# Layer norms' rows moved from VectorE to ScalarE, the second experts' gate made one SiLU, and new priorities for the order of the work

## What is computed

```python
h = _layernorm(x, axis=-1) * (1 + ca) + sa
x = x + ga * _L0_attn_ref(h, ...)      # 8 heads, top 20% of the scores emphasised
h = _layernorm(x, axis=-1) * (1 + cb) + sb
x = x + gb * _L0_ffn_ref(h, ...)       # two more layer norms inside, 8 experts, SiLU
...
h = _layernorm(x, axis=-1) * (1 + ca) + sa
x = x + ga * _L1_attn_ref(h, ...)      # state-space scan, 16 states
h = _layernorm(x, axis=-1) * (1 + cb) + sb
x = x + gb * _L1_ffn_ref(h, ...)       # 8 experts of limited capacity
```

```python
h = jnp.einsum('eti,eih->eth', einp2, w_c_fc) + b_c_fc
g = jnp.einsum('eti,eih->eth', einp2, w_gate) + b_gate
o = jnp.einsum('eth,eho->eto', jax.nn.silu(h * g), w_c_proj) + b_c_proj
```

## Time and profile before

| | us |
|---|---|
| median of 3 runs (lowest, highest) | 2912.05 (2910.93, 2914.12) |
| the profiled execution, whole | 2906.13 |
| its span in the trace | 2904.7 |
| DVE busy | 2341.4 (81%) |
| PE busy | 2152.1 (74%) |
| ACT busy | 1467.0 (51%) |
| POOL busy | 1193.4 (41%) |

### The profile page before, as it was taken

One profiled execution on the slowest core, in us unless ns is written; L12 is line 12 of the kernel. 1 busy time (PEld: TensorE's weight loads), 2 busy tenths in 40 slices (PEclk: granted clock), 3 DMA queues, 4 the chain that ended last, 5 costly groups with the idle time before them and its releaser, 6 DMA issues.

```text
span 2904.7 us, 33586 instructions
## 1 busy us (share of the span) xinstructions
PE 2152.1 (74%) x8658; PEld 1109.6 (38%) x8767; DVE 2341.4 (81%) x6145; ACT 1467.0 (51%) x3124; POOL 1193.4 (41%) x1118
## 2 busy tenths in 40 slices
PE   4168776978788876877778876878778787778644
PEld 2016322643244522553245522554235532454214
DVE  5974898988898898988898888988988887953472
ACT  3306814775276714765166723766156741744323
POOL 2020354515363353615454153814445163724461
PEclk8579898998989999998989899998979899889757
DMA  4011013232132313242142312233033321313223
GB/s 107 1 24 38 26 31 105 78 100 68 40 124 57 114 42 93 70 107 78 31 126 67 100 49 79 91 86 96 24 111 77 97 61 46 116 44 107 81 74 97
DMA packets 137459, 215.11 MB, mean 74 GB/s; under 512 B 17872, under 2 KB 57440, under 8 KB 134112
## 3 DMA queue, kind: packets, MB, share of 16 engines
q1 hardware_dynamic: 133088, 203.88, 24.8%
q0 software_dynamic: 4096, 8.40, 1.0%
HBM read 190.06 MB, written 22.15 MB: 73 GB/s over the span
## 4 chain that ended last, share of the span: by engine, by line
DVE 37%; issue 19%; PE 17%; POOL 11%; ACT 9%; DVEq 4%; another core or an unknown queue 2%; DMA 1%; SPq 0%; POOLq 0%; ACTq 0%
DVE wmask L819 9%; DVE best L961 6%; POOL gat L1670 4%; ACT wmask L801 4%; DVEq L963 4%; PE ps_att L1079 3%; POOL slots L1786 2%; POOL rest_c L1683 2%; DVE pick L968 1%; DVE xr L1914 1%; PE ps_rest L1457 1%; PE ps_att L1090 1%; PE ps_rest L1371 1%; PE ps_rest L1831 1%
## 5 line engine op out<-in xcount | busy, mean ns | idle before, releaser
L1431 POOL TENSOR_TENSOR gat<-sil,cbs 128x512 f32<-128x512 f32 x256 | 325.2, 1276 | 432.9 <-ACT sil L1396 371.2
L1396 ACT ACTIVATE sil<-ps_rest,w_b1T 128x512 f32<-128x512 f32 x256 | 175.4, 686 | 471.5 <-PE ps_rest L1371 438.1
L819 DVE TENSOR_SCALAR_CACHE_REDUCE wmask<-z,tc 128x512 bf16<-128x512 f16 x512 | 347.8, 740 | 17.4 <-ACT z L786 14.4
L1079 PE MATMUL ps_att<-z,Vp 128*32 128x128 f32 x2048 | 279.7, 283 | 39.2 <-DVE z L1151 25.2
L995 POOL TENSOR_SCALAR wmask<-wmask 128x512 bf16<-128x512 bf16 x256 | 159.0, 621 | 339.5 <-DVE wmask L952 335.6
L1361 PE MATMUL ps_rest<-gat,WP 128*128 128x512 f32 x512 | 269.5, 608 | 21.9 <-POOL gat L1431 21.8
L1371 PE MATMUL ps_rest<-rest_hT,WF 128*128 128x512 f32 x512 | 282.5, 638 | 0.3 <-ACT sil L1396 0.2
L1079 PEld LDWEIGHTS ps_att<-z,Vp 128*32 128x32 f32 x2048 | 208.5, 112 | 133.7 <-issue 104.6
L752 PE MATMUL ps_att<-qk 128*128 128x512 bf16 x473 | 201.7, 447 | 48.8 <-DMA qk<-bounce 27.1
L1590 PE MATMUL ps_rest<-hg,ident 128*128 128x512 f32 x256 | 176.3, 777 | 76.5 <-DVE hg L1642 75.0
L1613 ACT ACTIVATE ps_rest<-cols,Aneg 128x512 f32<-128x512 f32 x256 | 174.4, 685 | 108.6 <-DVE hg L1642 103.9
(11 more groups left out here) (357 smaller groups left out, 4786.3 us busy)
## 6 DMA issues: line engine op xcount, KB each, us to landing
cbs<-spreads SPq DMA_DIRECT2D x128, 256.0 KB, 3.7
ccs<-spreads SPq DMA_DIRECT2D x128, 256.0 KB, 3.4
WF<-in_w SPq DMA_DIRECT2D x64, 256.0 KB, 2.8
WP<-in_w SPq DMA_DIRECT2D x64, 256.0 KB, 2.7
WF<-in_wfc SPq DMA_DIRECT2D x64, 256.0 KB, 2.7
WG<-in_wgate SPq DMA_DIRECT2D x64, 256.0 KB, 3.0
WP<-in_wproj SPq DMA_DIRECT2D x64, 256.0 KB, 3.3
qk<-bounce SPq DMA_DIRECT2D x32, 384.0 KB, 5.1
```

The lines of the kernel that those rows point to most:

```text
L819: od.up(dve.tensor_scalar(wmask[:, i, :], z_at[i], tc[:, 0, i:i + 1], None, ALU.is_ge, ALU.add, accum_out=tc[:, 1, i:i + 1]))
L1079: mm = pe.matmul(obank[o:o + 32, a * P:(a + 1) * P], Vp[:, kc, h, :], pT[u][:, kc, :], start=kc == 0, stop=kc == NT - 1)
L1431: weighed0.up(pool.tensor_tensor(gat[m % 2], sil[m % 2], cbs[e % 2][:], ALU.mult))
```

## The change

Each norm's rows are now computed on ACT: out = Identity(rstd * x + away) with away = -mean * rstd. DVE writes -mean into a new small tile `away` (128x4), POOL multiplies it with rstd, and ACT makes four activations (in the new `act_rows`) with a scale and a bias per partition. DVE no longer waits for POOL in a norm. In the second experts one ACT instruction, SiLU of the product, stands where tanh stood; the DVE instruction behind it is gone, and gbh no longer has the factor of a half. The priorities have new values with four marks instead of three, PERIOD is -65.7 where it was 95.6, and NEAR is 0.152 where it was 0.114.

```diff
-PERIOD = 95.6
+PERIOD = -65.7
 TIMETABLE = {
...
-    "dve_rest": (104.8950, (5087.6, 8109.1, 5975.4)),
+    "dve_rest": (96.6350, (3916.6, 6668.4, 6271.0, 5222.1)),
...
+            self.away = sb(name + "_away", [P, NT])
...
-            self.var, self.rooted = sig(name + "_var", norms), sig(name + "_rooted", norms)
+            self.var, self.rooted = sig(name + "_var", 2 * norms), sig(name + "_rooted", 2 * norms)
...
         siluc.up(act.activation(Aneg[:], wts["A_log"][:], ACT.Exp))
+        for _ in act_rows(att, 0, 0, xr[0], att.nrm):
+            pass
...
-        gbs.up(dve.tensor_scalar(gbh[:], modT[1][:, :, 5], 0.5, None, ALU.mult))
+        gbs.up(dve.tensor_scalar(gbh[:], modT[1][:, :, 5], 1.0, None, ALU.mult))
...
-    def act_norm(w, b, k, bank, scale, shift, dst):
+    def act_rows(w, b, k, src, nrm):
+        yield w.rooted.at(b, 2 * k + 1)
+        act.wait_ge(*w.rooted.at(b, 2 * k + 1))
+        for j in range(NT):
+            w.normal.up(act.activation(nrm[:, j, :], src[:, j, :], ACT.Identity, bias=w.away[:, j:j + 1], scale=w.rstd[:, j:j + 1]))
+            yield 0.3
+
+    def act_norm(w, b, k, bank, scale, shift, dst, src=None, nrm=None):
+        if src is not None:
+            yield from act_rows(w, b, k, src, w.nrm if nrm is None else nrm)
         yield w.turned.at(b, k)
...
-    def dve_norm(w, b, k, src, nrm=None):
+    def dve_norm(w, b, k, src):
...
         w.var.up(dve.tensor_scalar(w.vpe[:], w.mv[:, :, 1], LN_EPS, None, ALU.add))
-        yield 0.21
-        yield w.rooted.at(b, k)
-        dve.wait_ge(*w.rooted.at(b, k))
-        for j in range(NT):
-            w.normal.up(dve.tensor_scalar((w.nrm if nrm is None else nrm)[:, j, :], src[:, j, :], w.mv[:, j, 0:1], w.rstd[:, j:j + 1],
-                                          ALU.subtract, ALU.mult))
-            yield 0.3
+        yield 0.1
+        w.var.up(dve.tensor_scalar(w.away[:], w.mv[:, :, 0], -1.0, None, ALU.mult))
+        yield 0.1
 
     def pool_norm(w, b, k):
-        yield w.var.at(b, k)
-        pool.wait_ge(*w.var.at(b, k))
+        yield w.var.at(b, 2 * k)
+        pool.wait_ge(*w.var.at(b, 2 * k))
         w.rooted.up(pool.tensor_tensor(w.rstd[:], w.vpe[:], halfs[:, 0:NT], ALU.pow))
         yield 1.06
+        yield w.var.at(b, 2 * k + 1)
+        pool.wait_ge(*w.var.at(b, 2 * k + 1))
+        yield w.rooted.at(b, 2 * k)
+        pool.wait_ge(*w.rooted.at(b, 2 * k))
+        w.rooted.up(pool.tensor_tensor(w.away[:], w.away[:], w.rstd[:], ALU.mult))
+        yield 0.25
...
-                tanhs.up(act.activation(acts[e % 2], prods[e % 2], ACT.Tanh, scale=0.5))
+                silus.up(act.activation(acts[e % 2], prods[e % 2], ACT.Silu))
...
-            if n >= 5 and (n - 5) % FC == 0 and (n - 5) // FC < E:
-                e = (n - 5) // FC
-                yield tanhs.at(b, e)
-                dve.wait_ge(*tanhs.at(b, e))
-                doubled.up(dve.scalar_tensor_tensor(acts[e % 2], acts[e % 2], 1.0, prods[e % 2], ALU.add, ALU.mult))
-                yield 0.73
...
-    NEAR = 0.114
+    NEAR = 0.152
```

84 lines of the change are left out of this document (42 added, 42 removed).

## The result

The changed kernel takes **2882.6 us** (median of 4 runs, 2879.6 to 2886.0) beside 2911.5 us for the kernel before on the same chip: a ratio of 0.9903, 95% interval 0.9886 to 0.9921, 28.9 us faster. The range (2755 to 2890) holds the time; the likeliest case doesn't. The gain is under a third of what was forecast.

The account below looks back on a forecast made before the run. DVE, 86% busy in the seven periods, was taken as the bound. Terms -91.3 - 16 + 20 - 4 - 3 = -94 us from 2906.1 gave 2812, and with 5.9 us for the median 2818 us; range 2755 to 2890.

Parts of the forecast that it names:

- the likeliest case: Whole launch: the main case, 2818 us with its own bounds 2780 to 2860, chance 0.62.
- The work that is moved: Seven periods: net 91.3 us off DVE, 11.4 us a period onto ACT, 49 table loads in the launch.
- All of it is DVE time in a stretch where DVE is the bound, so I take it whole: Seven periods: the main term, all 91.3 us net taken from DVE shorten the launch.
- I take a third of the 8.6 us ... 20 us in all; the bounds are 0 and 60: Search stage: a third of ACT's added time per period delays closings that wait for ACT, costing 20 us.
- DVE's waits for POOL, 16 us: Norms in the seven periods: half of DVE's 31.9 us idle waiting for POOL is gained, 16 us.
- I put 0, with 40 us on either side: Order from the new priorities: how well stages fit together changes nothing, within 40 us either way.
- Start and end: Before and after the seven periods: -4 us at the start, -3 us at the end.
- ACT becomes the bound of the search stage: Rival: the search stage keeps its 127 us, savings come only elsewhere, 2888 us; chance 0.16.
- Its mark: Search stage: DVE's waits for ACT at round closings doubled, DVE's share of the stage under 78%.
- The slower case: Rival: ACT stands before the norms' rows until POOL releases it, over 50 us; 2918 to 3002 us, chance 0.08.
- The last sign named: Whole launch: forecast wrong if DVE's busy time falls as said and its idle time grows by over half of it.

Follow-up runs that it names:

- e3: The kernel before in its own order, with DVE's gate product L1905 narrowed to 8 of 612 columns: 2899.3 us, ratio 0.9970.
- e9: The kernel before, order held still, with the gate alone changed (SiLU for tanh, no doubled product): 2905.2 us, ratio 0.9990.
- e11: The kernel before, order held still, with both edits (norms' rows on ACT, SiLU as the gate): 2936.5 us, ratio 1.0091.
- e4: The changed kernel in its own order, with plain tanh in SiLU's place, product left out, 34 table loads: 2866.1 us, ratio 0.9854.
- e14: The kernel before in its own order, with 188 unused 128x128 rows added on ACT behind the norms' rows: 2931.3 us, ratio 1.0070.
- e15: The changed kernel in its own order, with 188 unused 128x128 rows added on ACT behind the norms' rows: 2928.1 us, ratio 1.0066.
- e8: The changed kernel in its own order, with ACT's rows of the rest's norms using constants, not waiting for POOL: 2875.5 us, ratio 0.9893.
- e10: The kernel before, order held still, with the norms' rows alone moved to ACT: 2928.1 us, ratio 1.0070.
- e18: The changed kernel in its own order, with the rows of three of the six norms back on DVE: 2885.8 us, ratio 0.9924.
- e13: The changed kernel in its own order, with the old gate (tanh on ACT, doubled product on DVE): 2890.2 us, ratio 0.9941.
- e5: The changed kernel with PE's first experts due 500 earlier, which rewove the whole order: 3103.2 us, ratio 1.0682.

## Why the prediction was wrong

*The work that is moved: right.* DVE's busy time in the periods fell from 1997.9 to 1900.6 us, 97 where 91.3 were forecast; ACT's rose by 78.7 us where 7 x 11.4 = 80 were forecast; there are 49 loads. A row on ACT takes 0.41 us in the queue, not 0.36; POOL's product 0.21 us, not 0.26. In front of a table load 0.02 us are lost and not 0.2, which I misread: 331.32 + 0.19 is 331.51, and the load starts at 331.53. And not most of DVE's saved time lay in the search stages, but 43 of 114 us (705.4 to 662.0).

*"All of it is DVE time in a stretch where DVE is the bound, so I take it whole": the step that failed.* I read 86% of busy time and the largest share of the chain as a bound. Of 35 us taken from DVE in the kernel before a quarter arrived (e3); the gate alone, 40 us off DVE with its loads, changed nothing that can be measured (e9). With both edits and nothing else changed, 96 us came off DVE and the kernel was 26 us slower (e11). In the search stages ACT's time set the pace, 0.8 to 1.0 us for each us that it got, and 47 us off DVE did nothing against that; between them 29 us off DVE gave some 4 us (1228.6 to 1199.2 busy, e11). My rows held the warning: in the search stage ACT was as near to full, once its new work was in, as I wrote myself, and I looked only at the closings.

*"I take a third of the 8.6 us ... 20 us in all; the bounds are 0 and 60": mis-sized.* The loads alone cost 14 to 16 us (e4), and 70 us more on ACT cost 20 us in the kernel before, 68 us more 47 us in the changed one (e14, e15). For the 79 us that ACT got in the periods that is 23 to 55 us. In the search stage, for which I took the third, the share was 0.8 to 1.0 in the old order (e14, e9 to e11) and 0.5 for time added in the changed one (e15).

*DVE's waits for POOL, 16 us: no gain seen.* They moved to ACT (88.5 us in the launch), and with 35 us of that removed the time moved by 3 to 7 us (e8). No run takes this wait from DVE alone: e10 does, with the rows, and was 20 us slower.

*"I put 0, with 40 us on either side" for the order: wrong in size and outside its bounds.* It is worth 55 us (e11 against the changed kernel), 29 in the search stages and 36 between them in the profiled executions (which differ by 59), and without it the change would be a loss. With these numbers the sum runs: edits in the old order +26 us, new order -55 us, together -29 us.

*Start and end*: -4 us forecast, +1 measured; -3 us forecast, -6.7 measured.

*The rivals.* "ACT becomes the bound of the search stage" gave 2888 us, 5 us from the result. Its core is borne out by e14, e11 and e4: the stage went with ACT, and did so before the change. That its number comes so near is luck in part, since it let the stage keep its length, where it is 12 us longer over seven, and had no gain from the order. Its mark was wrong: the closings didn't wait longer (44.2 us), the chunks of the second experts did (116.1 us for 77.3), and DVE's share of the stage is 81%, not under 78%. The slower case's mark, ACT idle over 50 us in front of the rows, is there (88.5 us), yet taking 35 us of it away gave 3 to 7 (e8); in e10 and e11 the kernel is slower, but with DVE's queue free of the wait and ACT's time as the price. The last sign named, idle time on DVE grown by over half of what it saved, is there: 91 of 114 us.

**What stays open.** Why time taken off ACT in the form of three norms' rows gave nothing (e18), while the table loads gave most of their length (e4), was not settled. The stages suggest that DVE stands close behind ACT there, since e18 and e13 gave DVE what ACT lost; but the places differ too, and in e18 DVE waits again for POOL. What the lower clock adds to e10, e11, e14 and e15 is open. How the 55 us of the new order split into their causes was not tried beyond e5.

## What to carry to other kernels

A high busy share of an engine whose queue is interleaved by hand with three others is not yet a bound. Before work is moved off it, add a known time to each engine at the places concerned, with nobody waiting for it: the share that arrives tells which engine is tight at those places, and so does a part of the work made narrow. Read the result by stage: a share of 0.29 hid 0.86 in one stage and nothing in the others. Moving work between two engines so close needs a new order, which can be worth more than the work; judge the edit once with the order held still and once refitted.
